# All transpositions of a unit ahead of all its scores, in an attention and expert kernel on one core

## The chip, the cores and the metric

The kernel runs on one core of a Trainium2 chip. The metric is the device time of the program in microseconds (us), the median of several runs. TensorE (PE) does the matrix products, VectorE (DVE) and ScalarE (ACT) empty its accumulator banks and do the softmax, GpSimd (POOL) normalises and issues the indirect DMAs, SyncE (SP) issues the other DMAs. Each has a queue of its own that runs in order, and they wait for each other on semaphores.

## What is computed

A block of 16 sequences of 512 tokens with 256 features: layer norm, causal attention with 16 heads of 64, and beside it a feed-forward part with one shared expert and 16 routed ones, of which each token takes its two best. Cut to the part in which the change lies:

```python
xn = layernorm(x)                                     # x: (16, 512, 256)
q = einsum('btd,hdk->bhtk', xn, Wq); k, v alike        # 16 heads of 64
wei = einsum('bhqk,bhsk->bhqs', q, k) * 64 ** -0.5
wei = softmax(where(causal, wei, -inf), axis=-1)
out = einsum('bhqs,bhsv->bhqv', wei, v)
x = x + (out.transpose(0, 2, 1, 3).reshape(16, 512, -1) @ Wo + bo) + ffn(xn)
```

## The kernel before

A first stage (to about 200 us) normalises the input, transposes it, splits the weights in two parts of lower precision and chooses the experts. The rest is one stream, `stream`, with a loop over `STEPS`. A unit u is a pair of heads of one sequence: 8 units make a sequence, 128 the whole. All five engines run the same loop of units, each with its own written-out list of work. Where a unit is mentioned below it is counted from 0 by its transpositions.

Queries are handled in four tiles of 128 tokens, 3, 2, 1 and 0; because of the causal mask tile i has i + 1 blocks of keys. Tiles 3 and 1 form one group each, 2 and 0 share the group "20" (`PARTS`). In step u PE works on two units at once: it transposes the probabilities of unit u (`transposes`, line 829) and computes the scores of unit u + 1 (`scores`, line 842). The probabilities have one buffer, `probs` (`probs_moved` is the same memory under another type), so a tile of unit u must have been transposed before VectorE writes the scores of unit u + 1 to its place.

The path of the softmax goes round the engines. PE's scores; on VectorE `maximum` (L1098), which masks, takes the extreme and moves the scores to `probs`; on ScalarE `exponential` (L980), which also sums; on VectorE `invert` (L1104), once for tiles 3 and 1 and once for 2 and 0; on POOL `normalise` (L1307), four instructions for tiles 3 and 1 and four for 2 and 0; in the next unit PE's transpositions (L838), which wait for `norm_done`; ScalarE and VectorE copy each half of the transposed blocks to `probs_t` (`take_probs`, L973 and L1091). After the scores PE does the work of the routed experts (`ticks`, from unit 35 to 89), the projections k, v and q of unit u + 2 (L811, L824), the output projection (L879) and last `weigh` (L863), probabilities times values. ScalarE and VectorE start a unit with `split_out`, which empties the bank of the weighting of the unit before (L998, L1120).

POOL's queue in a unit holds `normalise` for tiles 3 and 1, in four units of each eight `prepare` (L1261, L1263), one part of `scatter` (L1270, two indirect DMAs, in units 2 to 33), `normalise` for 2 and 0, and the other part of the scatter. In the middle stretch it gathers expert weights (L1282), in the last one it gathers rows (L1298) that VectorE adds (L1189) at the end of a unit.

PE's results go to eight accumulator banks that are handed out in turn. `order` (line 608) lists the kinds of work of a unit in the order in which they take a bank; `take` waits until the work that held the bank eight takings earlier has been emptied. The list must have the same order as PE's work. SyncE paces its loads by `pace` (line 646), which waits for the count of finished transposition groups `t_ready` (3u + 1 and 3u + 3) and of projections.

Of the kernel before, what the change touches and what calls it, by code (L numbers as in the profile page):

```python
# [485 lines left out]
def stream(nc, ins, dram, keep, out):  # L486

    with ExitStack() as ctx:
        def sb(name, shape, dt=F32):
            return ctx.enter_context(nc.sbuf_tensor("d_" + name, shape, dt))  # L490
# [10 lines left out]
        v = [sb(f"v{r}", [P, QT, 2 * P]) for r in range(2)]  # L501
# [88 lines left out]
        def half(r):  # L590
            return slice(r * DK, (r + 1) * DK)

        def there(kind, u):
            if kind[0] == "s":
                return 0 <= u + 1 < UNITS
            if kind in "kqv":
                return u + 2 < UNITS
            if kind in ("gate", "up"):
                return 0 <= u < UNITS and u % PAIRS == 1
            return 2 <= u < UNITS + 2 if kind == "o" else 0 <= u < UNITS  # L600

        def tick(u, part):
            n = TICKS.get((u, part))
            if n is None:
                return {}
            return {kind: n - back for kind, back in (("dn", 2), ("gu", 1), ("xt", 0)) if 0 <= n - back < SLOT_TILES}

        def order(u):

            kinds = ["t3", "t3", "t1", "t1", "s3", "s3", "s1", "s1", "t20", "t20", "s20", "s20", 0, "k", "v", "gate", "q",  # L610
                     "o", "up", 1, "w"]
            for n, kind in enumerate(kinds):
                if kind in (0, 1):
                    for each, t in tick(u, kind).items():
                        yield each, 0, t
                elif there(kind, u):
                    yield kind, (int(kinds[n - 1] == kind) if kind[0] in "st" else 0), u
# [25 lines left out]
        with nc.Block() as block:  # L643
# [154 lines left out]
            def _(pe):  # L798
                def take(kind, u, r=0):
                    at, free = banks[kind, r, u]  # L800
                    if free is not None:
                        pe.wait_ge(*free)
                    return ring[at]
# [25 lines left out]
                def transposes(fill, u):  # L829
                    to = [take(f"t{fill}", u, r) for r in range(2)]  # L830
                    pe.wait_ge(norm_done, 8 * u + NTH[PARTS[fill][-1][0], 1] + 1)
                    slots = sum(i + 1 for i, _ in PARTS[fill])
                    for i, at in PARTS[fill]:
                        for h in range(2):
                            for j in range(i + 1):
                                for r in range(2):
                                    off = (h * slots + at + j) * DK
                                    last = pe.transpose(to[r][:, off:off + DK].bitcast(F32R),  # L838
                                                        moved[half(r), i, h, j * P:(j + 1) * P], ident[half(r), half(r)])
                    last.then_inc(t_ready, 1)  # L840

                def scores(fill, u):
                    to, r = [take(f"s{fill}", u, h) for h in range(2)], (u + 1) % 2
                    pe.wait_ge(p_out, 2 * (u + 1) + 2)
                    for i, at in PARTS[fill]:
                        cols = (i + 1) * P
                        for n, (qa, kb) in enumerate(PASSES):
                            for h in range(2):
                                last = pe.matmul(to[h][:, at * P:at * P + cols], qs[r][qa][half(h), i * P:(i + 1) * P],  # L849
                                                 ks[r][kb][half(h), 0:cols], start=(n == 0), stop=(n == len(PASSES) - 1))  # L850
                    last.then_inc(s_ready, 1)
# [79 lines left out]
                def ticks(u, part):  # L931
                    n = tick(u, part)
                    if "dn" in n:
                        slot_down(n["dn"])
                    if "gu" in n:
                        slot_expand(n["gu"])
                    if "xt" in n:
                        slot_transposes(n["xt"])

                for u in STEPS:  # L940
                    attends = 0 <= u < UNITS
                    if attends:
                        transposes(3, u)
                        transposes(1, u)
                    if there("s3", u):
                        scores(3, u)
                        scores(1, u)
                    if attends:
                        transposes(20, u)
                    if there("s20", u):  # L950
                        scores(20, u)
                    ticks(u, 0)
                    if there("k", u):
                        project("k", u)
                        project_v(u)
                    if there("gate", u):
                        expand("gate", u)
                    if there("q", u):
                        project("q", u)
                    if there("o", u):  # L960
                        project_out(u)
                    if there("up", u):
                        expand("up", u)
                    ticks(u, 1)
                    if attends:
                        weigh(u)
# [120 lines left out]
            def _(dve):  # L1087
                def take_probs(fill, u):
                    dve.wait_ge(t_ready, 3 * u + FILL[fill] + 1)
                    slots = probs_t[fill].shape[2]  # L1090
                    dve.tensor_copy(probs_t[fill][:, :, :, half(1)], bank(f"t{fill}", u, 1)[:, 0:2 * slots * DK].rearrange(  # L1091
                        "p (h j n) -> p h j n", h=2, n=DK)).then_inc(t_out[1], 1)
# [99 lines left out]
                for u in STEPS:  # L1192
                    attends, ahead = 0 <= u < UNITS, there("s3", u)
                    if 0 <= u - 1 < UNITS:
                        split_out(u - 1)
                    if attends:
                        take_probs(3, u)
                        take_probs(1, u)
                    if ahead:
                        maximum(3, 0, u)  # L1200
                        maximum(3, 1, u)
                    if attends:
                        take_probs(20, u)
                    if ahead:
                        maximum(1, 0, u)
                        maximum(1, 1, u)
                        maximum(2, 0, u)
                        maximum(2, 1, u)
                        maximum(0, 0, u)
                        maximum(0, 1, u)  # L1210
                        invert(31, u + 1)
                    n = tick(u, 0)
                    if "gu" in n:
                        slot_gate(n["gu"])
                        slot_widen(n["gu"])
                    if "xt" in n:
                        split_xt(n["xt"])
                    if there("k", u):
                        split_projected("k", u)
                    if "gu" in n:  # L1220
                        split_slots(n["gu"])
                    if there("v", u) and u % 2:
                        take_v(u)
                    if there("gate", u):
                        gate(u)
                    if there("q", u):
                        split_projected("q", u)
                    if ahead:
                        invert(20, u + 1)
                    if there("o", u):  # L1230
                        add_out(u)
                    if there("up", u):
                        widen(u)
                    if u in PACK_AT:
                        split_pack(PACK_AT[u])
                    done = [m for m, item in enumerate(ITEMS) if item[0] == u - 1]
                    n = tick(u, 1)
                    if "gu" in n:
                        slot_gate(n["gu"])
                        slot_widen(n["gu"])  # L1240
                    if "xt" in n:
                        split_xt(n["xt"])
                    if there("up", u):
                        split_hidden(u)
                    if "gu" in n:
                        split_slots(n["gu"])
                    for part in range(2):
                        for m in done:
                            add_routed(m, part)
# [138 lines left out]
```

## Time and profile before

| what | value |
|---|---|
| median of 3 runs | 2040.12 us (2039.69 to 2041.51) |
| the profiled execution | 2039.6 us |
| its span, first to last instruction | 2037.9 us |
| PE busy | 1892.4 us, 93% |
| VectorE, ScalarE, POOL busy | 69%, 59%, 50% |
| mean granted clock of TensorE | 0.965 |

The profile is of one execution. Busy time of an engine is a share of the whole span; a stretch must be read for itself. In the rows below a line of a timeline has the start in us, the length in us, the engine, the line of the kernel, the operation, output and input, their shapes and "xN" for N instructions in a row; what stands in brackets is the idle time of the engine before it and who ended it. The end of the last matmul of a row overlaps the start of the next, so lengths of PE's work are taken from start to start.

### The profile page before, as it was taken

Reading aid. Unit: us, or ns where it says so; the run is one execution under the profiler, and the core shown is the slowest. Engines: PE = TensorE matmul, PEld = TensorE weight load, DVE = VectorE, ACT = ScalarE, POOL = GpSimd, SP = SyncE. Lnnn points to the kernel's source line nnn. Section 1 sums busy time; section 2 is a strip of 40 time slices with the busy share of each in tenths; the row PEclk is TensorE's granted clock in tenths of the full one; section 3 lists DMA queues with packets and bytes.
Section 4 is the critical chain, followed back from the end, with each engine's and each line's share of the span. In section 5 each row is a group of like instructions: output and inputs, shape, how many; then the busy total and the mean of one; then the engine's idle time right before and its main releaser. Section 6 shows DMA issues by size and latency. Waiting matters only on the chain.

```text
span 2037.9 us, 53480 instructions
## 1 busy us (share of the span) xinstructions
PE 1892.4 (93%) x20356; PEld 1720.7 (84%) x20356; DVE 1409.7 (69%) x4091; ACT 1205.8 (59%) x3328; POOL 1018.4 (50%) x1515
## 2 busy tenths in 40 slices
PE   4641999999999999999999999999999999999998
PEld 2430898989888899999999999999999989888897
DVE  4667666666666666666676666667666887888865
ACT  2222666666666566666666666666666666655564
POOL 0004467776766343443433434334343777777752
PEclk9765999999999999999999999999999999999999
DMA  9878243434342354434544345453442334333210
GB/s 273 291 298 338 66 143 123 148 125 147 125 146 90 125 156 135 146 128 148 164 133 156 120 148 154 139 160 118 155 136 69 109 102 118 110 112 103 89 33 12
DMA packets 162196, 284.95 MB, mean 140 GB/s; under 512 B 27552, under 2 KB 113312, under 8 KB 157344
## 3 DMA queue, kind: packets, MB, share of 16 engines
q1 hardware_dynamic: 135264, 164.16, 25.6%
q0 software_dynamic: 23808, 96.49, 14.4%
q10 hardware_dynamic: 2880, 20.97, 2.5%
q8 instruction: 163, 2.67, 0.6%
q14 instruction: 81, 0.66, 0.1%
HBM read 169.36 MB, written 112.20 MB: 138 GB/s over the span
## 4 chain that ended last, share of the span: by engine, by line
PE 70%; POOL 11%; issue 6%; ACT 1%; DVE 1%; DMA 0%; POOLq 0%; SPq 0%; DVEq 0%
PE d_bank L811 14%; PE d_bank L863 11%; PE d_bank L849 10%; PE d_bank L838 9%; PE d_bank L824 7%; POOL d_probs L1307 7%; PE d_bank L879 7%; PE d_bank L917 6%; POOL queued_rows L1270 4%; PE d_bank L904 3%; PE d_bank L895 2%; PE d_bank L927 1%; ACT d_probs L980 1%; PE d_bank L884 1%; POOL d_base L1261 1%
## 5 line engine op out<-in xcount | busy, mean ns | idle before, releaser
L1307 POOL TENSOR_SCALAR d_probs<-d_probs,d_inverse 128x512 f32<-128x512 f32 (+3 forms) x1024 | 546.6, 549 | 740.5 <-DVE d_inverse L1104 738.9
L980 ACT ACTIVATE d_probs<-d_probs,d_bias 128x512 f32<-128x512 f32 (+3 forms) x1024 | 561.0, 552 | 1.2 <-DVE d_bias L1098 1.2
L811 PE MATMUL d_bank<-d_xnt,wqk_all 128*128 128x512 f32 x1536 | 414.8, 406 | 41.1 <-DMA d_xnt<-xnt_split 41.1
L1098 DVE CUSTOM_DVE_ANT_0 d_probs<-d_bank,mask 128x512 f32<-128x512 f32 (+3 forms) x1024 | 439.0, 485 | 1.9 <-PE d_bank L849 1.8
L811 PEld LDWEIGHTS d_bank<-d_xnt,wqk_all 128*128 128x128 f32 x1536 | 274.3, 190 | 96.5 <-DMA d_xnt<-xnt_split 42.0
L849 PE MATMUL d_bank<-d_ks,d_qs 64*128 64x512 f32 (+3 forms) x3072 | 313.1, 333 | 8.7 <-issue 6.8
L863 PE MATMUL d_bank<-d_probs_t,d_v 128*64 128x128 f32 x5120 | 310.3, 276 | 0.0
L973 ACT ACTIVATE d_probs_t<-d_bank 128x512 f32<-128x512 f32 (+1 forms) x384 | 188.9, 526 | 205.1 <-PE d_bank L838 205.0
L863 PEld LDWEIGHTS d_bank<-d_probs_t,d_v 128*64 128x64 f32 x5120 | 279.2, 138 | 15.8 <-issue 3.8
L849 PEld LDWEIGHTS d_bank<-d_ks,d_qs 64*128 64x128 f32 x3072 | 250.4, 186 | 27.9 <-issue 10.9
L838 PE MATMUL d_bank<-ident_r,d_probs_moved 64*128 64x64 f32 x5120 | 255.8, 244 | 9.4 <-POOL d_probs L1307 9.3
L838 PEld LDWEIGHTS d_bank<-ident_r,d_probs_moved 64*128 64x128 f32 x5120 | 232.4, 135 | 36.4 <-issue 35.1
L1109 DVE TENSOR_TENSOR d_qs<-d_bank,d_qs 128x512 fp32r<-128x512 f32 x128 | 88.5, 692 | 210.7 <-ACT d_qs L986 210.7
L1091 DVE COPY d_probs_t<-d_bank 128x512 f32<-128x512 f32 (+1 forms) x384 | 217.3, 594 | 4.9 <-PE d_bank L838 4.5
L998 ACT ACTIVATE d_out_t<-d_bank 128x512 fp32r<-128x512 f32 x128 | 76.6, 598 | 240.0 <-PE d_bank L863 240.0
L824 PEld LDWEIGHTS d_bank<-wv_all,d_xnt 128*128 128x128 f32 x1536 | 201.6, 192 | 11.1
L879 PEld LDWEIGHTS d_bank<-wo_all,d_out_t 128*128 128x128 f32 x1536 | 200.3, 189 | 12.2 <-issue 1.7
L879 PE MATMUL d_bank<-wo_all,d_out_t 128*128 128x256 f32 x1536 | 206.0, 280 | 1.5 <-DVE d_out_t L1120 1.5
L824 PE MATMUL d_bank<-wv_all,d_xnt 128*128 128x256 f32 x1536 | 203.4, 283 | 0.0
L980 ACT ACTIVATION_READ_ACCUMULATOR d_probs<-d_probs,d_bias 128x1 f32 x1024 | 195.0, 190 | 0.0
L1120 DVE TENSOR_TENSOR d_out_t<-d_bank,d_out_t 128x512 fp32r<-128x512 f32 x128 | 88.3, 690 | 123.4 <-ACT d_out_t L998 123.2
L1298 POOL DMA_INDIRECT d_rows<-routed_rows,slot x128 | 132.5, 1035 | 35.6 <-issue 34.0
(126 smaller groups left out, 2258.9 us busy)
## 6 DMA issues: line engine op xcount, KB each, us to landing
queued_rows<-a_zeros ACTq DMA_DIRECT2D x20, 1024.0 KB, 17.4
d_x<-queued_rows SPq DMA_DIRECT2D x80, 256.0 KB, 3.8
routed_rows<-d_y SPq DMA_DIRECT2D x80, 256.0 KB, 4.2
xnt_split<-a_xnt SPq DMA_DIRECT2D x16, 1024.0 KB, 4.2
d_xnt<-xnt_split SPq DMA_DIRECT2D x64, 256.0 KB, 3.6
expert_rows<-d_w SPq DMA_DIRECT2D x32, 384.0 KB, 3.5
a_x_in<-in_L_attn_x SPq DMA_DIRECT2D x16, 512.0 KB, 4.9
xn_rows<-a_xn SPq DMA_DIRECT2D x16, 512.0 KB, 5.5
```

Of the source, the lines that this page charges most:

```text
L811: last = pe.matmul(to[:, :], wqk[:, n % PAIRS, "qk".index(kind), wa, k, :], xnt[n // PAIRS % 2][:, xb, k, :], start=first, stop=(k == KD - ...
L824: last = pe.matmul(to[:, t * 2 * P:(t + 1) * 2 * P], xnt[b % 2][:, xa, k, tok * P:(tok + 1) * P], wv[:, wb, k, cols], start=(k == 0 and (x ...
L838: last = pe.transpose(to[r][:, off:off + DK].bitcast(F32R), moved[half(r), i, h, j * P:(j + 1) * P], ident[half(r), half(r)])
L849: last = pe.matmul(to[h][:, at * P:at * P + cols], qs[r][qa][half(h), i * P:(i + 1) * P], ks[r][kb][half(h), 0:cols], start=(n == 0), stop ...
L863: last = pe.matmul(to[half(h), i * P:(i + 1) * P], v[u // 2 % 2][:, j, col:col + DK], probs_t[fill][:, h, at + j, :], start=(j == 0), stop ...
L879: last = pe.matmul(to[:, s * D:(s + 1) * D], out_t[g % 2][oa][:, j, cols], wo[:, wb, g % 4 * GROUP + j, :], start=(j == 0 and n == 0), sto ...
L973: act.activation(probs_t[fill][:, :, :, half(0)], bank(f"t{fill}", u)[:, 0:2 * slots * DK].rearrange("p (h j n) -> p h j n", h=2, n=DK), A ...
L980: act.activation(part, part, ACT.Exp, bias=bias[:, i, h:h + 1], scale=-1.0, accum_out=total[which][:, at % 4:at % 4 + 1]).then_inc(exp_don ...
L1091: dve.tensor_copy(probs_t[fill][:, :, :, half(1)], bank(f"t{fill}", u, 1)[:, 0:2 * slots * DK].rearrange("p (h j n) -> p h j n", h=2, n=DK ...
L1098: dve.tensor_tensor_reduce(out=probs[:, i, h, 0:cols], in0=bank(f"s{fill}", u, h)[:, at * P:at * P + cols], in1=mask[:, T - cols:T], scale ...
L1298: pool.indirect_dma_start(out=rows[m % 4 // 2][:, m % 2 * 2 + n, :], out_offset=None, in_=dram["routed"][:, :], in_offset=bass.IndirectOff ...
L1307: pool.tensor_scalar(part, part, inverse[which][:, at % 4:at % 4 + 1], 1.0, ALU.mult, ALU.mult).then_inc(norm_done, 1)
```

## The change

In each unit the transpositions of group 20 move ahead of the scores of groups 3 and 1, on PE and in the list that hands out the banks. VectorE's copy of the transposed group 20 moves ahead of the first two maxima. ScalarE's list (which already copied all three groups before the exponentials), POOL's and SyncE's are unchanged, and so are the instructions themselves.

```diff
@@ order @@
-            kinds = ["t3", "t3", "t1", "t1", "s3", "s3", "s1", "s1", "t20", "t20", "s20", "s20", 0, "k", "v", "gate", "q",
+            kinds = ["t3", "t3", "t1", "t1", "t20", "t20", "s3", "s3", "s1", "s1", "s20", "s20", 0, "k", "v", "gate", "q",
                      "o", "up", 1, "w"]
@@ tensor @@
                     if attends:
                         transposes(3, u)
                         transposes(1, u)
+                        transposes(20, u)
                     if there("s3", u):
                         scores(3, u)
                         scores(1, u)
-                    if attends:
-                        transposes(20, u)
-                    if there("s20", u):
                         scores(20, u)
@@ vector @@
                     if attends:
                         take_probs(3, u)
                         take_probs(1, u)
+                        take_probs(20, u)
                     if ahead:
                         maximum(3, 0, u)
                         maximum(3, 1, u)
-                    if attends:
-                        take_probs(20, u)
-                    if ahead:
                         maximum(1, 0, u)
```

## Rows read from the trace of the kernel before

**Rows 1.** The page: busy times of the engines.
```profile
PE 1892.4 (93%) x20356; PEld 1720.7 (84%) x20356; DVE 1409.7 (69%) x4091; ACT 1205.8 (59%) x3328; POOL 1018.4 (50%) x1515
```

**Rows 2.** Waits: who waited for whom; us in total, times, longest.
```profile
POOL d_probs L1307 <- DVE d_inverse L1104: 738.9, 198, 10.8
...
PE d_bank L838 <- POOL d_probs L1307: 9.3, 14, 2.2
```

**Rows 3.** Windows, PE alone: stretch, length, busy (instructions), clock, DMA share, GB/s.
```profile
228.20:679.10 450.90, 441.76 (x5002) 0.99 0.38 126
679.10:1561.20 882.10, 882.10 (x9626) 1.00 0.44 140
1561.20:2022.00 460.80, 453.19 (x5150) 0.99 0.30 88
```

**Rows 4.** Timeline of unit 38, in the middle: PE's transpositions and scores, POOL's normalisations.
```profile
705.99 1.85 POOL L1307 TENSOR_SCALAR d_probs<-d_probs,d_inverse 128x384 f32<-128x384 f32 x4 [1.11 <-DVE d_inverse L1104]
...
711.24 1.17 PE L838 MATMUL d_bank<-ident_r,d_probs_moved 64*128 64x64 f32 x24
...
712.25 1.32 PE L849 MATMUL d_bank<-d_ks,d_qs 64*128 64x512 f32 x12
...
713.39 0.83 PE L838 MATMUL d_bank<-ident_r,d_probs_moved 64*128 64x64 f32 x16
...
714.03 1.10 PE L849 MATMUL d_bank<-d_ks,d_qs 64*128 64x384 f32 x12
...
715.06 0.98 PE L904 MATMUL d_bank<-d_w,d_slot_hs 128*128 128x256 f32 x6
...
717.69 2.27 POOL L1307 TENSOR_SCALAR d_probs<-d_probs,d_inverse 128x512 f32<-128x512 f32 x4 [8.57 <-DVE d_inverse L1104]
```

**Rows 5.** Timeline at the head of the stream: the first scores, nothing transposed yet.
```profile
208.01 2.13 PE L849 MATMUL d_bank<-d_ks,d_qs 64*128 64x512 f32 x24 [1.41 <-DVE d_qs L1109]
...
209.74 0.72 ACT L980 ACTIVATE d_probs<-d_probs,d_bias 128x512 f32<-128x512 f32 x1 [1.22 <-DVE d_bias L1098]
210.06 1.65 PE L811 MATMUL d_bank<-d_xnt,wqk_all 128*128 128x512 f32 x6
...
212.58 2.29 POOL L1307 TENSOR_SCALAR d_probs<-d_probs,d_inverse 128x512 f32<-128x512 f32 x4 [9.04 <-DVE d_inverse L1104]
```

**Rows 6.** Timeline of units 7 and 8: a held t20 and what follows it.
```profile
302.50 1.17 PE L838 MATMUL d_bank<-ident_r,d_probs_moved 64*128 64x64 f32 x24
...
305.29 0.84 PE L838 MATMUL d_bank<-ident_r,d_probs_moved 64*128 64x64 f32 x16 [0.48 <-POOL d_probs L1307]
...
306.66 0.71 ACT L980 ACTIVATE d_probs<-d_probs,d_bias 128x512 f32<-128x512 f32 x1
...
309.47 2.28 POOL L1307 TENSOR_SCALAR d_probs<-d_probs,d_inverse 128x512 f32<-128x512 f32 x4 [1.80 <-DVE d_inverse L1104]
...
315.03 1.17 PE L838 MATMUL d_bank<-ident_r,d_probs_moved 64*128 64x64 f32 x24
...
315.79 1.84 POOL L1307 TENSOR_SCALAR d_probs<-d_probs,d_inverse 128x384 f32<-128x384 f32 x4
...
317.78 0.83 PE L838 MATMUL d_bank<-ident_r,d_probs_moved 64*128 64x64 f32 x16 [0.43 <-POOL d_probs L1307]
```

**Rows 7.** Timeline of unit 11: POOL's last normalisations and the first transpositions.
```profile
354.10 2.46 POOL L1307 TENSOR_SCALAR d_probs<-d_probs,d_inverse 128x384 f32<-128x384 f32 x4
...
354.71 1.17 PE L838 MATMUL d_bank<-ident_r,d_probs_moved 64*128 64x64 f32 x24
```

**Rows 8.** Timeline and windows of units 112 and 113: two gaps of PE and the clock.
```profile
1827.16 0.63 PE L849 MATMUL d_bank<-d_ks,d_qs 64*128 64x256 f32 x6 [1.46 <-issue]
...
1841.53 0.63 PE L849 MATMUL d_bank<-d_ks,d_qs 64*128 64x256 f32 x6 [1.99 <-issue]
...
1827.20:1837.50 10.30, 10.30 (x110) 1.00 0.60 180
...
1843.70:1847.10 3.40, 3.40 (x13) 0.50 0.34 90
```

## The prediction, made before the changed kernel was built

> **What bounds the kernel now.** I read the page first: TensorE is busy 93% of the span, no other engine more than 69%, GpSimd (POOL) 50% [rows 1]. The list of waits then says who stops whom. POOL waits 738.9 us for the reciprocals, so it has time on average; TensorE waits for POOL's normalised probabilities only 9.3 us in 14 places [rows 2]. Cut in three by windows, TensorE (PE) has no idle time at all from 679.1 to 1561.2 us (units 36 to 90), and 9.1 and 7.6 us of it before and after [rows 3]. So there are two regimes. In the middle only PE's own work counts. In units 1 to 35 (POOL also scatters rows there) and in some of the last 37, a wait at the transpositions sets the pace, and the question is how much margin POOL leaves.
>
> I call S the start of the first transposition of a unit u, and T the end of POOL's last normalisation of query tiles 2 and 0, which group t20 transposes. t31 and t20 are the transpositions of tiles 3, 1 and of 2, 0; s31 and s20 are the scores of unit u+1.
>
> **PE's own work.** In a unit with nothing to wait for, t31, s31, t20, s20 start at 711.24, 712.25, 713.39, 714.03 and the next work at 715.06 [rows 4]: 1.01 + 1.14 + 0.64 + 1.03 = 3.82 us. The number of instructions doesn't change. The trace has one place where both score groups already run in one go, at the head of the stream: 24 score matmuls from 208.01 to 210.06 = 2.05 us [rows 5], against 1.14 + 1.03 = 2.17. Against that, t20 after t31 costs its full rate, 16/24 of 1.01 = 0.67 instead of 0.64. Saved: 0.12 - 0.03 = 0.09, and I take 0.08 us per unit (a seam between transpositions and scores gone). Bounds: 0 (the seam only moves) and 0.12. This is all there is in units 36 to 90: 55 x 0.08 = 4.4 us. Nothing waits there in the new order: the normalisation that t20 needs began at 705.99 and took 1.85, so T = 707.84, 3.4 us before S = 711.24 [rows 4].
>
> **t20 comes 1.15 us earlier.** It now starts at S + 1.00, not S + 2.15. In unit 7, S = 302.50; t20 started at 305.29 and was held 0.48 us by POOL, and in unit 8 (S = 315.03) T = 315.79 + 1.84 = 317.63 with t20 at 317.78, 0.15 after T [rows 6]. In unit 11, S = 354.71 and T = 354.10 + 2.46 = 356.56, S + 1.85 [rows 7]: before, it fits under s31; now it doesn't. That cover, 1.15 us of s31 work ahead of t20, is what the change removes.
>
> **The loop gets longer as well.** What follows t20? VectorE now has the copy of t20 ahead of the first two maxima, and PE has s31 behind t20. So while t20 waits for POOL, s31, the maxima and the exponentials queue behind it on PE, VectorE and ScalarE. Before, s31 and the maxima of tile 3 ran during the wait: from t20 at 305.29 the first exponential came at 306.66 and the first normalisation of tiles 3 and 1 (call it N) at 309.47, t20 + 4.18 [rows 6]. Now it is t20 (0.67), then s31, maxima, exponentials. At the head of the stream scores at 208.01 led to the first exponential at 209.74 and to N at 212.58, 4.57 later [rows 5]. So N = t20 + 0.67 + 4.57 = t20 + 5.24; I take 5.22 (bounds: 4.18, if something still hides the maxima, and 5.45). Where nothing waits, N stays at S + 6.45: it was 717.69 - 711.24 = 6.45 there, set by VectorE's unbroken run of the same copies and maxima, only in another order. From N to the next T is POOL's own queue (normalise, add to base, two scatters, normalise): 309.47 to 317.63 = 8.16 in the three units of a batch in which it adds to base before the scatters [rows 6], 6.7 to 7.3 in the others. A bound unit then lasts 5.22 + 8.16 + 0.15 = 13.5 us, where it was 4.17 + 8.16 + 0.15 = 12.5 (315.03 - 302.50 = 12.53), and where PE's own work is 11.9.
>
> **The sum for one batch of eight units.** Rule now: t20 = larger of S + 1.00 and T + 0.14; N = larger of S + 6.45 and t20 + 5.22; next T = N + POOL's queue; next S = t20 + PE's own length - 1.00 - 0.08. With 2.15, 4.17 and no 0.08 the same rule gives back the measured starts of units 1 to 31 within 0.03 us. Units 10 to 17, read as in rows 6 and 7: T - S is 0.20, 1.85, 1.16, 1.13, 0.44, 2.75, 2.61, 2.62; PE's own length 11.87, 11.95, 12.59, 12.65, 11.87, 11.88, 11.88, 14.73; POOL's queue 7.27, 6.67, 7.28, 6.66, 8.19, 8.16, 8.18, 8.59. The waits come out at 0, 1.08, 0.16, 0.20, 0, 1.98, 1.72, 1.74 = 6.9 us, against 0.75 + 0.59 + 0.60 = 1.9 now. Less 8 x 0.08 = 0.6: +4.3 us a batch. The same line by line for units 1 to 35: +17.6 (+15.8 with 5.0, +21.0 with 5.45, +11.7 with 4.18). Unit 0 behaves alike, its t20 waited for POOL, and s31 and its chain now come after that: +1.0.
>
> **Units 91 to 127.** 36 x 0.08 = -2.9. In a few of them s1 waits for the bank of the weighting, which VectorE empties late (idle 1.46 and 1.99 us) [rows 8]. The bank order shifts: that bank now goes to s3. Ahead of it PE then has t31 and t20, 1.67 us, where it had t31 and s3, about 1.7, so that wait stays as long. By the same rule t20 is held a little in five of these units (estimate +0.9), and about as much falls away where t20 waited for the bank of t3, which now goes to s1 (-1.0). SyncE's loads are paced by the end of t20, which comes earlier: no cost. POOL's instructions are the same in the same order.
>
> **The granted clock.** An idle 1.46 us of PE was followed by a stretch at full clock, 1.99 us by 3.4 us at half clock (0.50, that is 1.2 instead of 2.4 GHz) [rows 8]. The new order makes some eleven gaps of 1.5 to 1.8 us. If six of them bring a half-speed stretch, each takes 1.7 us of PE work, most of which lies in units that would wait for POOL anyway; I charge 0.7 each: +4 (0 to 19).
>
> Sum against the profiled execution (2039.6 us, 1.7 outside its span of 2037.9): 17.6 + 1.0 - 4.4 - 2.9 - 0.1 + 4 = +15. The median of the runs is 2040.1, so 2055.
>
> **Rivals.** (A) Faster: PE is the bound throughout, and t20's earlier place costs nothing. 127 x 0.08 = -10: 2030. It decides at T = S + 0.86: if POOL is done by then everywhere, no wait appears. For it: 738.9 us of POOL idle and 55 units with 3 us of margin. Against: T = S + 1.85 and S + 2.6 in the rows. The Trainium skill, "Perfetto Trace Analysis", section Identifying the Most-Contended Engine, says in the same spirit that improving the engine in highest demand generally improves the kernel; by that rule alone the time would be the 2030 of this rival. [...] (B) No measurable change: the chain after t20 keeps its 4.18 and the seams give 0.12 instead of 0.08: 11.7 + 1.0 - 91 x 0.12 - 36 x 0.04 = +0.3, some 2040. Against: VectorE's order is written out, the copy stands ahead of the maxima. (C) The clock makes it worse: all eleven gaps cost their full 1.7 us: 11.3 + 18.7 = +30, 2070.
>
> **How the numbers follow.** The forecast has 0.73, A 0.06, B 0.07, C 0.14. The forecast's own ends: no clock loss, a chain of 5.0 and 0.12 saved give 2046; 5.45, no seam gain (21.8 in the early units) and 4 us of clock give 2067. To leave out less than 0.2 the range goes to C: 2045 to 2070. A measurement of this kernel can tell a change of some 0.2% (4 us) from none. Faster 0.07 (A and a little of B), same 0.06, slower 0.87.
>
> **What would show it.** TensorE's wait for POOL's normalisation goes from 9.3 to some 30 to 36 us; the window from unit 36 to unit 91 shrinks from 882.1 to about 877.7 us; unit 36 starts near 698 to 702 instead of 679.1; bound units last 13.5 us; from t20 to N it is 5.2 us there; half-clock stretches appear in units 7 to 34. I am wrong if t20 isn't held in unit 11, if N stays 4.2 behind a held t20, or if the middle window gets longer.

## The result and the profile after

The changed kernel takes 2055.8 us (median of 4 runs, 2054.9 to 2058.6), the kernel before 2039.9 on the same chip; the ratio is 1.0079 with a 95% interval of 1.0062 to 1.0096. It is slower by 16 us. The profiled execution took 2055.55 us with a span of 2053.8. TensorE's wait for the normalisation, 9.3 us in 14 places in [rows 2], is now 32.7 in 25, and ScalarE has a wait that it hardly had before (1.2 us), for VectorE's maxima; its wait for the transposed blocks fell meanwhile from 205.0 to 67.4 us (line numbers behind the change are lower by 2 to 4):

```profile
POOL d_probs L1303 <- DVE d_inverse L1102: 752.9, 206, 9.4
...
ACT d_probs L978 <- DVE d_bias L1096: 150.0, 128, 2.9
...
PE d_bank L838 <- POOL d_probs L1303: 32.7, 25, 3.5
```

Windows of PE, cut at the starts of units 0, 36, 91 and 127 (columns as in [rows 3]), say where the time went, and the last one shows the clock behind the hold in unit 7:

```profile
212.62:702.14 489.52, 461.04 (x5129) 0.97 0.37 121
702.14:1578.42 876.28, 876.28 (x9626) 1.00 0.44 141
1578.42:2035.92 457.50, 448.85 (x5126) 0.99 0.30 89
305.60:312.40 6.80, 6.17 (x43) 0.52 0.22 68
```

The same cuts of all profiled executions, each from the first transposition of a unit to that of another. "Half clock" counts the stretches in which the granted clock was at its lower level in units 0 to 35 (the windows of the trace at 0.50):

| kernel | units 0-35 | 36-90 | 91-126 | half clock | median of runs, ratio to before (95%) |
|---|---|---|---|---|---|
| before | 464.7 | 882.1 | 458.8 | 3 | 2039.9 |
| changed | 489.5 | 876.3 | 457.5 | 8 | 2055.8, 1.0079 |
| VectorE's list undone (e1) | 496.4 | 881.5 | 456.2 | 10 | 2068.2, 1.0153 (1.0136 to 1.0169) |
| VectorE's list alone (e2) | 488.6 | 912.6 | 479.8 | 7 | 2113.4, 1.0371 (1.0355 to 1.0387) |
| new order in 36-90 only (e3) | 462.7 | 876.3 | 456.9 | 3 | 2030.4, 0.9967 (0.9954 to 0.9979) |
| new order, scatters last (e4) | 455.2 | 876.3 | 457.9 | 2 | 2021.1, 0.9915 (0.9902 to 0.9928) |
| old order, scatters last (e5) | 452.8 | 881.9 | 459.1 | 2 | 2025.7, 0.9948 (0.9934 to 0.9963) |
| three rounds (e6) | 485.9 | 930.1 | 488.2 | 2 | 2133.2, 1.0468 (1.0448 to 1.0488) |
| changed, filler products (e7) | 478.9 | 876.3 | 458.0 | 0 | 2044.2, 1.0031 (1.002 to 1.0041) |
| changed, filler transpositions (e8) | 483.4 | 876.3 | 457.6 | 4 | 2049.5, 1.0056 (1.0036 to 1.0077) |
| new order but four units, scatters last (e9) | 452.1 | 876.3 | 456.4 | 1 | 2019.1, 0.9905 (0.9888 to 0.9921) |

The kernel before was timed again beside each group of experiments: 2037.7 us beside e1 to e4, 2035.2 beside e5 and e6, 2038.0 beside e7 to e9. Medians of different groups are therefore compared by their ratios. The cuts are of one execution each. Where the code of a stretch is the same they still differ by some 2 us: before and e3 have the same code in units 0 to 35 (464.7 and 462.7; the half-clock stretch of unit 31 lasted 6.8 us in one and 3.4 in the other).

So the change costs 24.8 us in units 0 to 35, brings 5.8 in the middle and 1.3 late, and 1.8 us come from the stage ahead of the stream, which it doesn't touch and which differs between executions: 24.8 - 5.8 - 1.3 - 1.8 = 15.9.

Unit 38 in the middle answers to [rows 4]. There 40 transpositions in one run take 733.89 to 735.55 = 1.66 us, 24 scores 2.06, together 3.72 where it was 3.82:

```profile
733.89 1.83 PE L838 MATMUL d_bank<-ident_r,d_probs_moved 64*128 64x64 f32 x40
...
735.55 2.12 PE L849 MATMUL d_bank<-d_ks,d_qs 64*128 64x512 f32 x24
...
737.61 0.98 PE L904 MATMUL d_bank<-d_w,d_slot_hs 128*128 128x256 f32 x6
```

Unit 11 answers to [rows 7], and shows what follows a held t20:

```profile
360.95 2.47 POOL L1303 TENSOR_SCALAR d_probs<-d_probs,d_inverse 128x384 f32<-128x384 f32 x4
361.47 1.17 PE L838 MATMUL d_bank<-ident_r,d_probs_moved 64*128 64x64 f32 x24
...
363.57 0.83 PE L838 MATMUL d_bank<-ident_r,d_probs_moved 64*128 64x64 f32 x16 [0.93 <-POOL d_probs L1303]
...
364.21 2.15 PE L849 MATMUL d_bank<-d_ks,d_qs 64*128 64x512 f32 x24
364.44 0.69 DVE L1089 COPY d_probs_t<-d_bank 128x512 f32<-128x512 f32 x1 [0.60 <-PE d_bank L838]
...
365.23 0.69 DVE L1096 CUSTOM_DVE_ANT_0 d_probs<-d_bank,mask 128x512 f32<-128x512 f32 x1
...
365.97 0.73 ACT L978 ACTIVATE d_probs<-d_probs,d_bias 128x512 f32<-128x512 f32 x1 [0.93 <-DVE d_bias L1096]
...
368.80 2.28 POOL L1303 TENSOR_SCALAR d_probs<-d_probs,d_inverse 128x512 f32<-128x512 f32 x4 [2.87 <-DVE d_inverse L1102]
```

POOL ends at 363.42, S + 1.95. PE is held 0.93 us with nothing to do, where in the kernel before s31 covered that time. Behind the hold all waits in a row: scores 0.64 us after t20's start, the first maximum at 1.66, the first exponential at 2.40, N at 5.23.

### The profile page after: what moved, and what is told of

It reads as the page before. It is cut to its first block, busy times and chain, and to the rows that moved or that the text cites. A ratio compares the mean times of both kernels' runs of the same rounds, so it can differ in the third digit from the quotient of the medians.

```text
span 2053.8 us, 53480 instructions
## 1 busy us (share of the span) xinstructions
PE 1887.3 (92%) x20356; PEld 1723.8 (84%) x20356; DVE 1415.5 (69%) x4091; ACT 1221.7 (59%) x3328; POOL 1022.6 (50%) x1515
## 4 chain that ended last, share of the span: by engine, by line
PE 62%; POOL 16%; issue 8%; DVE 4%; ACT 1%; DMA 0%; POOLq 0%; SPq 0%; DVEq 0%
PE d_bank L811 12%; PE d_bank L849 9%; PE d_bank L863 9%; POOL d_probs L1303 9%; PE d_bank L838 7%; PE d_bank L879 6%; PE d_bank L824 6%; PE d_bank L917 6%; POOL queued_rows L1266 4%; PE d_bank L904 3%; DVE d_probs L1096 2%; PE d_bank L895 2%; POOL d_rows L1294 1%; PE d_bank L927 1%; PE d_bank L884 1%
## 5 line engine op out<-in xcount | busy, mean ns | idle before, releaser
L1096 DVE CUSTOM_DVE_ANT_0 d_probs<-d_bank,mask 128x512 f32<-128x512 f32 (+3 forms) x1024 | 430.7, 486 | 8.2 <-PE d_bank L849 6.6
L849 PE MATMUL d_bank<-d_ks,d_qs 64*128 64x512 f32 (+3 forms) x3072 | 288.0, 335 | 3.9 <-issue 2.5
L838 PEld LDWEIGHTS d_bank<-ident_r,d_probs_moved 64*128 64x128 f32 x5120 | 225.5, 136 | 59.3 <-issue 59.0
L838 PE MATMUL d_bank<-ident_r,d_probs_moved 64*128 64x64 f32 x5120 | 242.9, 245 | 33.9 <-POOL d_probs L1303 32.7
L849 PEld LDWEIGHTS d_bank<-d_ks,d_qs 64*128 64x128 f32 x3072 | 256.7, 195 | 18.7 <-issue 2.9
L971 ACT ACTIVATE d_probs_t<-d_bank 128x512 f32<-128x512 f32 (+1 forms) x384 | 188.4, 525 | 78.6 <-PE d_bank L838 67.4
L1089 DVE COPY d_probs_t<-d_bank 128x512 f32<-128x512 f32 (+1 forms) x384 | 207.8, 592 | 21.9 <-PE d_bank L838 21.8
```

Of the source, the lines that this page charges most:

```text
L838: last = pe.transpose(to[r][:, off:off + DK].bitcast(F32R), moved[half(r), i, h, j * P:(j + 1) * P], ident[half(r), half(r)])
L971: act.activation(probs_t[fill][:, :, :, half(0)], bank(f"t{fill}", u)[:, 0:2 * slots * DK].rearrange("p (h j n) -> p h j n", h=2, n=DK), A ...
L1096: dve.tensor_tensor_reduce(out=probs[:, i, h, 0:cols], in0=bank(f"s{fill}", u, h)[:, at * P:at * P + cols], in1=mask[:, T - cols:T], scale ...
```

## The experiments

The theory: (1) t20 lost the cover of s31 and is held where POOL is late; (2) s31 and the softmax now queue behind the held t20, so each hold lengthens the way to the next one; (3) PE itself saves 0.1 us per unit; (4) half-clock stretches follow the longer holds.

**Which of the two lists does it.** First VectorE's list as it was, with PE's new order:

```diff
                         take_probs(1, u)
-                        take_probs(20, u)
                     if ahead:
                         maximum(3, 0, u)
                         maximum(3, 1, u)
+                    if attends:
+                        take_probs(20, u)
+                    if ahead:
```

> The changed kernel with VectorE's list put back as it was (copy of t20 behind the first two maxima); PE's order and the banks stay changed. Theory (s31 stands behind t20 on PE, and the first maximum waits for it): the change's price stays. From a held t20 to the first normalisation it is still 5.2 us, because the scores of tile 3 end some 1.7 us after t20 starts while the copy would be done at 1.5. Where t20 isn't held, VectorE now waits for s3, so that distance S to N grows from 6.45 to some 6.8. Time 2055 to 2060. Rival (VectorE's copy ahead of the maxima makes the chain long): N falls back to 4.2 us behind a held t20 and the time to 2050 or less.

It took 2068.2 us. By the ratios that is some 15 us more than the changed kernel, against 0 to 5 expected. Unit 11 of it:

```profile
364.98 0.83 PE L838 MATMUL d_bank<-ident_r,d_probs_moved 64*128 64x64 f32 x16 [0.67 <-POOL d_probs L1305]
...
366.65 0.69 DVE L1096 CUSTOM_DVE_ANT_0 d_probs<-d_bank,mask 128x512 f32<-128x512 f32 x1 [1.14 <-PE d_bank L849]
...
367.88 0.69 DVE L1089 COPY d_probs_t<-d_bank 128x512 f32<-128x512 f32 x1
...
370.81 1.37 POOL L1305 TENSOR_SCALAR d_probs<-d_probs,d_inverse 128x512 f32<-128x512 f32 x2 [3.47 <-DVE d_inverse L1102]
```

The first maximum still comes 1.67 us after t20, because it waits for the scores. The copy isn't what delays it, so the rival falls. But N comes at t20 + 5.83, not 5.2: VectorE stands still for 1.14 us and has the copy left to do behind the maxima, ahead of the reciprocal. The expectation had this effect where t20 isn't held (S to N 6.84, 6.8 expected) and overlooked it where it is. It also missed 5.2 us in the middle (881.5): t20's banks go to the next work on PE, and VectorE now copies its half late. In unit 40 that copy ends at 776.63 + 0.69 = 777.32, and the products that take its bank start at 777.37, 0.92 us behind the group ahead of them instead of 0.81. VectorE's half of the change is thus a help; with PE's new order the copy belongs ahead.

Then VectorE's list alone, on the kernel before:

```diff
                         take_probs(1, u)
+                        take_probs(20, u)
                     if ahead:
                         maximum(3, 0, u)
                         maximum(3, 1, u)
-                    if attends:
-                        take_probs(20, u)
-                    if ahead:
```

> The kernel before with only VectorE's list changed (copy of t20 ahead of the first two maxima); PE keeps its two rounds, so t20 starts at S + 2.15 as before. Theory: VectorE now stands still for t20 while s31 is long done. From t20 to N it is some 5.1 us instead of 4.2, held or not, and S to N grows from 6.45 to some 7.2. By the recurrence of the prediction units 1 to 35 get 13 us longer, PE's own work is unchanged (882 us in units 36 to 90): 2053. Rival (only t20's earlier place on PE costs): 2040.

It took 2113.4 us, 60 more than expected. The two distances were right: N comes 5.02 us after t20 (5.1 expected) and 7.18 after S (7.2). What was missed is in PE's queue. In the middle, at 790.88:

```profile
787.51 1.32 PE L849 MATMUL d_bank<-d_ks,d_qs 64*128 64x512 f32 x12
...
789.29 1.10 PE L849 MATMUL d_bank<-d_ks,d_qs 64*128 64x384 f32 x12
789.52 0.69 DVE L1091 COPY d_probs_t<-d_bank 128x512 f32<-128x512 f32 x1 [0.64 <-PE d_bank L838]
790.13 0.68 DVE L1098 CUSTOM_DVE_ANT_0 d_probs<-d_bank,mask 128x512 f32<-128x512 f32 x1
...
790.88 1.65 PE L811 MATMUL d_bank<-d_xnt,wqk_all 128*128 128x512 f32 x6 [0.48 <-DVE d_bias L1098]
```

The work after s20 takes the bank that s3 had eight takings earlier. The first maximum empties it, and it now comes too late by 0.48 us in each unit: 46.2 us in 96 places before k and 12.6 us in 26 before the routed work in the list of waits. In the changed kernel the same work takes the bank of t20, which is copied early. PE's order, VectorE's list and the order of banks only work as a set.

**The new order where POOL is early.** `TOGETHER = range(36, 91)`; outside it, PE, banks and VectorE keep the old order.

> The new order only in units 36 to 90, where POOL is done 3 us before a unit begins; the old order in all others. Theory (two regimes): the stretch before unit 36 and the one from unit 91 take as long as in the kernel before, and the middle loses 0.10 us per unit, 5.8 us as in the changed kernel: 2034. Rival (the gain of the middle is lost again, since what it saves turns into waits behind unit 90): 2038 to 2040.

It took 2030.4 us, 0.9967 of the time before: 6.7 us less, where 5.8 were expected. The middle is 876.3 us as in the changed kernel, and nothing is given back behind it (456.9). The late stretch, whose code is that of the kernel before, differs from it by 1.9 us here, so the 1.3 us that the changed kernel gains there can't be told from no gain.

**POOL in time.** The changed kernel with

```diff
-                    if u in SCATTER_AT:
-                        scatter(*SCATTER_AT[u], 0)
                     if there("s20", u):
                         for i in (2, 0):
                             for h in range(2):
                                 normalise(i, h, u + 1)
+                    if u in SCATTER_AT:
+                        scatter(*SCATTER_AT[u], 0)
```

> The changed kernel, and on POOL the first part of the scatter moves behind the normalisation of tiles 2 and 0, so that T comes some 2.4 us earlier in units 3 to 34. Theory (the cost is POOL's lateness at t20, nothing else): T - S falls to about 0.2 in the units of a batch with the additions to base and below 0 in the others, no t20 is held there, the half-clock stretches of units 7 to 33 go, and only the 0.10 us per unit stay: 2019, that is 37 less than the changed kernel and 21 less than the one before. Rival (the new order is slow in itself, by PE or VectorE): 2045 or more. Rival (POOL is now late with the normalisation of tiles 3 and 1, which queues behind four scatters): N moves from S + 6.45 to later, 2025 to 2035.

It took 2021.1 us (2019 expected), some 33 less than the changed kernel by the ratios. Units 0 to 35 go from 489.5 to 455.2 us. In unit 11, S = 353.41:

```profile
352.06 2.54 POOL L1303 TENSOR_SCALAR d_probs<-d_probs,d_inverse 128x384 f32<-128x384 f32 x4 [1.71 <-DVE d_inverse L1102]
...
353.41 1.17 PE L838 MATMUL d_bank<-ident_r,d_probs_moved 64*128 64x64 f32 x24
...
354.75 0.84 PE L838 MATMUL d_bank<-ident_r,d_probs_moved 64*128 64x64 f32 x16 [0.16 <-POOL d_probs L1303]
```

A hold of 0.16 us is left, in three units of a batch. What sets T here is no longer the scatters: POOL waits 1.71 us for the reciprocals, and its four instructions then take 2.54 us; with 1.84, their time in other units, t20 wouldn't be held. So it wasn't quite "no t20 held", but half clock in units 7 to 33 is gone and POOL isn't late with tiles 3 and 1 (S to N 6.44 or 6.57). The same move with the old order:

> The kernel before with the same move on POOL alone (first part of the scatter behind the normalisation of tiles 2 and 0). Theory: the eleven waits of t20 in units 1 to 35 go (9.1 us) and with them the half-clock stretch of unit 31 (2.6 us), PE's own work is as before: 2028. Against the same move in the changed kernel this gives the worth of the new order where POOL is in time: 9 us, 0.10 us per unit and less in the units that were held. Rival (the scatters aren't what makes POOL late): 2038 to 2040.

It took 2025.7 us (2028 expected). From the two ratios the new order is then worth 0.33%, some 7 us; from the cuts it brings 5.6 in the middle and costs 2.5 in units 0 to 35 (1.4 of it in units 0 and 1, 1.0 in unit 35). In units 2 to 34, from the first start to the last end, the two orders take 409.7 and 409.5 us: the small holds eat what the order saves there. Its worth lies in the middle, where POOL has time. The sign of the change is POOL's doing: with the scatters ahead of the normalisation the new order costs 16 us, with them behind it saves some 7.

**The seam.** The kernel before with one more change of kind: t3, s3, t1, s1, t20, s20.

```diff
                         transposes(3, u)
-                        transposes(1, u)
                     if there("s3", u):
                         scores(3, u)
+                    if attends:
+                        transposes(1, u)
+                    if there("s3", u):
                         scores(1, u)
```

> The kernel before with one more change between transpositions and scores on PE: t3, s3, t1, s1, t20, s20. Theory (0.10 us per unit is the price of one seam): a unit of the middle takes 3.92 us from its first transposition to the end of s20, where it is 3.82 in two rounds and 3.72 in one; units 36 to 90 last 882.1 + 5.5 = 888 us. t20 starts 0.1 us later, so the held units change by little: 2046 to 2049. Rival (what was saved is not the seam but that s20 follows s1 or that a bank is free earlier): the middle stays at 882 us.

It took 2133.2 us and is no clean test of the seam. A unit of the middle:

```profile
784.98 0.83 PE L838 MATMUL d_bank<-ident_r,d_probs_moved 64*128 64x64 f32 x16
785.65 0.96 PE L849 MATMUL d_bank<-d_ks,d_qs 64*128 64x512 f32 x6
786.45 0.43 PE L838 MATMUL d_bank<-ident_r,d_probs_moved 64*128 64x64 f32 x8
786.71 0.62 PE L849 MATMUL d_bank<-d_ks,d_qs 64*128 64x256 f32 x6
787.16 0.79 PE L838 MATMUL d_bank<-ident_r,d_probs_moved 64*128 64x64 f32 x16
788.66 1.08 PE L849 MATMUL d_bank<-d_ks,d_qs 64*128 64x384 f32 x12 [0.72 <-DVE d_bias L1100]
```

The bank list moved with the order, s20 now takes the banks of s3, and PE waits 0.72 us for a maximum in each unit (87.1 us in 125 places). Without that wait the added seam is small: t3 to the start of t20 is 2.18 us, where t31 and s31 took 2.15, so +0.03 and not +0.10. A seam thus has no fixed price. Removing the one ahead of s20 saved 0.10, adding one between groups 3 and 1 cost 0.03. What makes the difference stays open.

**The clock.** The changed kernel, with PE given work in the holds of units 0 to 33, into the bank of t20 that is overwritten afterwards; what it computes isn't used:

```diff
                         transposes(1, u)
+                        spare = [take("t20", u, r) for r in range(2)] if u in FILLER else None
+                        for _ in range(FILLER.get(u, 0)):
+                            pe.matmul(spare[0][:, 0:256], wqk[:, 0, 0, HI, 0, :], wv[:, HI, 0, 0:256],
+                                      start=True, stop=True)
                         transposes(20, u)
```

> The changed kernel, in which PE works during the hold of t20: in units 0, 3, 7 to 9, 11, 15 to 17, 19, 23 to 25, 27 and 31 to 33 it runs 8 to 28 more products of 128x128 by 128x256 into the bank of t20 before t20 overwrites it, some 0.9 to 3 us of work that is shorter than the hold. They give nothing that is used. Theory (part of the early stretch's cost is the half clock that follows the holds): the half-clock stretches at units 7, 9, 15, 17, 23, 31 and 33 go, and units 0 to 35 last some 481 us (the recurrence without a clock term) instead of 489.5: 2047. Rival (the clock costs nothing, since PE waits for POOL anyway): the half-clock stretches go and the time stays at 2055. Rival (the fillers come to stand in the way): longer.

It took 2044.2 us (2047 expected). By the ratios that is some 10 us less than the changed kernel, with 214 more products to run. In unit 7 a hold of 1.83 us became 0.18, and the clock stays up. The two rows are first of the changed kernel, then of this one:

```profile
306.23 1.21 PE L838 MATMUL d_bank<-ident_r,d_probs_moved 64*128 64x64 f32 x16 [1.83 <-POOL d_probs L1303]
307.22 3.81 PE L849 MATMUL d_bank<-d_ks,d_qs 64*128 64x512 f32 x24
```

```profile
302.79 1.70 PE L951 MATMUL d_bank<-wv_all,wqk_all 128*128 128x256 f32 x12
304.67 0.83 PE L842 MATMUL d_bank<-ident_r,d_probs_moved 64*128 64x64 f32 x16 [0.18 <-POOL d_probs L1311]
305.31 2.15 PE L853 MATMUL d_bank<-d_ks,d_qs 64*128 64x512 f32 x24
...
303.00:313.00 10.00, 9.82 (x88) 1.00 0.26 80
```

No half clock is left in units 0 to 35, N comes 5.2 us after every held t20, and these units last 478.9 us instead of 489.5. So 10.6 us of them were the clock's (in units 11, 19 and 27 the filler ends 0.2 us too late, so it is rather more). The same with pairs of transpositions as filler:

> As the kernel with filler products, but the fillers are pairs of transpositions of the identity (64 rows, as those of the kernel), as long in sum (10 to 36 pairs of 0.083 us). If any work of PE keeps the clock, this is as fast as the one with products, 2047. If transpositions don't, as the Trainium skill has it (TensorE: Matmul & The Clock Gate, section Part 4: PE-mode transpose, which says that a transposition doesn't count as busy in the same way), the half-clock stretches stay and the time is that of the changed kernel, 2055.

It took 2049.5 us, between the two: four half-clock stretches (in units 0, 15, 31 and 33) instead of eight or none, 483.4 us. One of them, in unit 15:

```profile
412.30:415.70 3.40, 3.40 (x32) 0.50 0.33 116
```

Transpositions thus did less than products. The Trainium skill says of them (TensorE: Matmul & The Clock Gate, section Part 4: PE-mode transpose) that they don't count as busy in the same way. The trace agrees in part: four stretches are left, but four of the changed kernel are gone as well. But this filler was also shorter (1.43 us against 1.70 in unit 7, with 0.54 us idle behind it), so the two causes aren't told apart.

**A version that beats both.** The new order with the scatters last, and the old order in units 0, 112, 113 and 120:

> The changed kernel with the scatters last on POOL, and with the old order in the four units in which t20 was still held for over 2 us (0, 112, 113, 120). Theory: unit 0 gives back 1.0 us, the others the difference between a hold of 2.2 us and the 1.5 to 2.0 us of the kernel before, some 1 us together: 2019, against 2021 for the new order in all units. Rival (those holds are set by POOL's own queue and only move): the same time as with the new order in all units.

It took 2019.1 us, 0.9905 of the time before (0.9888 to 0.9921), against 0.9915 (0.9902 to 0.9928) without the four units. As expected in size, but the intervals overlap, so the last step isn't shown. Together with the one that has the new order in all units it is the fastest kernel of this study.

## Why the prediction was right

It said 2055 with a range of 2045 to 2070; 2055.8 was measured. The signs that it named came: TensorE's wait for the normalisation is 32.7 us (30 to 36 said), unit 36 starts at 702.1 (698 to 702), and the middle window shrinks. By its steps:

- PE's own work: 0.08 us per unit was taken from a choice between 0 and 0.12; it is 0.10. Both parts of the estimate were good (scores 2.05 expected, 2.06 measured; 40 transpositions 1.01 + 0.67 = 1.68 expected, 1.66 measured), and the rest is the rounding of 0.09 down to 0.08. The middle gave 5.8 us instead of 4.4.
- The lost cover: t20 held in unit 11, yes, 0.93 us idle.
- The longer loop: from a held t20 to N 5.22 predicted, 5.23 measured. The row that carried this was the head of the stream [rows 5], where scores already ran without transpositions. S + 6.45 where nothing is held: 6.44.
- The sum without a clock: 17.6 + 1.0 us predicted, some 18.9 measured. The changed kernel with the clock held up takes 478.9 us. The kernel before has three half-clock stretches of its own in these units, and their cost has to come off first. The one of unit 31 costs 2.6 us by the recurrence. The one of unit 35 costs 1.3: the weighting takes 3.66 us there from start to start, and 2.34 in the changed kernel, where the same idle time was followed by none. The one of unit 0 costs 1.5 us, taken from the changed kernel (t20 to the next unit 10.95 us there, 9.39 with the clock held up); of these the recurrence gives back 0.7 in unit 1, which waits less for POOL. That leaves 460.0 us, an estimate. The rows of units 35 and 0, first of the kernel before, then of the changed one:

```profile
675.02 0.51 PE L927 MATMUL d_bank<-ident_r,d_x 128*128 128x128 f32 x4 [2.22 <-DMA d_x<-queued_rows]
675.46 3.72 PE L863 MATMUL d_bank<-d_probs_t,d_v 128*64 128x128 f32 x40
...
219.00:222.40 3.40, 3.40 (x21) 0.50 1.02 348
676.40:679.80 3.40, 3.40 (x40) 0.50 0.00 0
```

```profile
699.37 0.51 PE L927 MATMUL d_bank<-ident_r,d_x 128*128 128x128 f32 x4 [2.22 <-DMA d_x<-queued_rows]
699.81 2.40 PE L863 MATMUL d_bank<-d_probs_t,d_v 128*64 128x128 f32 x40
```

- The clock: +4 us predicted, some +5.9 measured (10.6 us lost now, 4.7 before). This is the term that was too small. The count was good: six units of 7 to 33 have a stretch that they hadn't before (7, 9, 15, 17, 23, 33); unit 31 had one already, twice as long, and the one of unit 35 fell away. The charge of 0.7 us each was not: the eight stretches cost 10.6 us, 1.3 each. The step behind it is "most of which lies in units that would wait for POOL anyway". Units 7, 8 and 9 last 16.59, 12.03 and 17.84 us in the changed kernel and 13.75, 13.53 and 16.28 with the clock held up. In unit 7 t20 and all 24 scores run at half clock, and N comes 6.49 us after t20 instead of 5.23. Unit 8 gives back 1.5 of the 2.8 us that unit 7 loses, because its own hold gets shorter; the delay of N is not given back. In unit 9 the stretch lies behind N, but the unit's own PE work is longer than POOL's way round (T of unit 10 is 1.6 us before S), so no later wait absorbs its 1.6 us.
- Units 91 to 126: -3.0 predicted, -1.3 measured, a difference within what the stretch differs by itself. Two places lose the seam's gain. In units 95 to 97 the scores start at S + 1.9 to 2.1 and not 1.67, as the bank of the weighting isn't free or t20 is held; the step "so that wait stays as long" didn't come true there. And units 111 to 121 take 151.4 us before and 151.5 now, with half clock of 10.2 us in two stretches before and 13.6 in four now.
- 1.8 us of the result are the stage before the stream.

Predicted less measured, the errors are -0.3 (recurrence), -1.9 (clock), +1.4 (middle), -1.7 (late) and +1.8 (first stage), and they nearly cancel. The mechanism is shown by e4 and e7. That the sum comes within 0.8 us is luck: the stage ahead of the stream, which no step speaks of, is 1.8 us of it, and the same code differs by 2 us from one execution to the next. Rivals: A (PE is the bound throughout) is wrong for the kernel and right for the middle, which e3 uses alone. B fails on N at 5.23. C assumed 18.7 us more for the clock; it was 5.9.

## What to carry to other kernels

Work that stands ahead of a wait is its cover: before gathering work of one kind to save switches, read how late the awaited engine is (here T - S, unit by unit) and what queues behind the wait. Where several engines go round a loop, a hold costs twice, once itself and once through what it delays for the next round; here a recurrence of four measured distances gave 18.6 us for both, where some 18.9 were measured. Banks handed out in turn tie the order of one engine to that of the engines that empty them, so half of such a change can be far worse than the whole. And if a reorder is worth 0.1 us a unit but loses it to a late engine, mend the late engine's queue first: here that cost one moved call.

## What the runs showed of the hardware

A short idle time of PE was enough to be followed by a half-clock stretch, but not each time. In the changed kernel 1.83 us in unit 7 had 6.8 us at the lower level behind it and 1.61 us in unit 9 had 3.4 us; another hold of 1.61 us, in unit 25, was followed by none. The idle 2.22 us at the end of unit 35 was followed by 3.4 us of half clock in the kernel before and by none in the changed one. The half clock cost 10.6 us in units 0 to 35, and useless products in the holds, which leave no work out, won it back.
